# A macaron transformer block on one core: setup in pieces, loop in another order, z of the first groups made in the loop

## The reference

```python
def fp4_quant_dequant(x):
    xb = x.reshape(shape[:-1] + (shape[-1] // BLOCK, BLOCK))
    scale = jnp.max(jnp.abs(xb), axis=-1, keepdims=True) / 6.0
    scale = jnp.maximum(scale, jnp.float32(1e-12))
    idx = jnp.searchsorted(_MID, jnp.abs(xb / scale))
    q = _GRID[idx] * jnp.sign(xb / scale) * scale
...
h = silu(fp4_linear(x, w_gate)) * fp4_linear(x, w_up)   # 256 -> 704
ffn = fp4_linear(h, w_down)                             # 704 -> 256
...
x = x + 0.5 * ffn(layernorm(x))
x = x + attention(layernorm(x))     # causal softmax, one head, d = 256
x = x + 0.5 * ffn(layernorm(x))
```

## Time and profile before

| | |
|---|---|
| median of 3 runs | 1227.78 us (1227.09 to 1229.02) |
| the profiled execution | 1227.53 us, its span 1225.4 us |
| TensorE busy | 1160.7 us, 95% |
| VectorE busy | 1012.5 us, 83% |
| ScalarE busy | 789.4 us, 64% |
| GpSimd busy | 555.3 us, 45% |
| TensorE idle, 0 to 80 us | 36.8 us |
| TensorE idle, 360 to 440 us | 12.9 us |

### The profile page before, as it was taken

One profiled execution on the slowest core, in us unless ns is written; L12 is line 12 of the kernel. 1 busy time (PEld: TensorE's weight loads), 2 busy tenths in 40 slices (PEclk: granted clock), 3 DMA queues, 4 the chain that ended last, 5 costly groups with the idle time before them and its releaser, 6 DMA issues.

```text
span 1225.4 us, 24518 instructions
## 1 busy us (share of the span) xinstructions
PE 1160.7 (95%) x7765; PEld 758.2 (62%) x7765; DVE 1012.5 (83%) x2809; ACT 789.4 (64%) x1599; POOL 555.3 (45%) x531
## 2 busy tenths in 40 slices
PE   1799999999998889999999999999999999999997
PEld 1356666666665656676677667566666666666665
DVE  6899999999999676557556654764799999999996
ACT  4678888888864444435544453665678888888862
POOL 1445544545443344435443444445344544545532
PEclk9899999999999999999999999999999999999999
DMA  6955455444444456556573656547355555555565
GB/s 208 254 95 97 85 97 96 84 89 91 90 91 80 89 114 110 106 118 106 106 130 81 119 101 120 111 90 122 59 102 115 109 115 122 114 110 113 111 124 114
DMA packets 462740, 134.35 MB, mean 110 GB/s; under 512 B 441296, under 2 KB 461904, under 8 KB 462672
## 3 DMA queue, kind: packets, MB, share of 16 engines
q1 hardware_dynamic: 454928, 125.62, 52.9%
q10 hardware_dynamic: 7744, 7.86, 2.0%
HBM read 11.34 MB, written 8.39 MB: 16 GB/s over the span
## 4 chain that ended last, share of the span: by engine, by line
PE 75%; DVE 12%; issue 4%; ACT 3%; DMA 2%; SPq 2%; POOL 1%; DVEq 0%; ACTq 0%; POOLq 0%
PE ps L1512 32%; PE ps L1471 17%; PE ps L1559 12%; PE ps L1547 10%; PE ps L1532 2%; PE ps L1525 2%; DMA arena<-arena 2%; SPq L436 2%; DVE arena L1156 1%; DVE arena L1135 1%; DVE arena L991 1%; DVE arena L987 1%; ACT arena L815 1%; DVE arena L1048 1%; DVE arena L1143 1%
## 5 line engine op out<-in xcount | busy, mean ns | idle before, releaser
L1512 PE MATMUL ps<-wguT,arena 128*128 128x512 f16 (+1 forms) x2304 | 479.5, 363 | 4.4 <-DMA arena<-arena 3.2
L1512 PEld LDWEIGHTS ps<-wguT,arena 128*128 128x128 f16 x2304 | 226.0, 98 | 224.9 <-issue 7.2
L567 POOL TENSOR_TENSOR arena<-arena 128x704 f32<-128x704 f32 x128 | 193.6, 1512 | 248.1 <-DVE arena L1000 248.1
L1471 PE MATMUL ps<-wdT,arena 128*128 128x256 f16 x2176 | 261.3, 275 | 13.8 <-DMA arena<-arena 6.8
L1471 PEld LDWEIGHTS ps<-wdT,arena 128*128 128x128 f16 x2176 | 213.6, 98 | 55.1 <-DVE x_sb L1058 9.1
L594 POOL TENSOR_TENSOR arena<-arena 128x128 f16<-128x128 f32 (+7 forms) x64 | 144.0, 2250 | 213.8 <-ACT arena L815 138.7
L824 ACT ACTIVATE arena<-ps,arena,cst 128x128 f16<-128x128 f32 (+7 forms) x64 | 80.5, 1257 | 172.1 <-DVE arena L1161 149.3
L1559 PE MATMUL ps<-arena 128*128 128x256 f16 x1632 | 188.7, 273 | 1.6 <-DVE x_sb L1174 1.6
L1547 PE MATMUL ps<-arena 128*128 128x512 f16 (+3 forms) x960 | 187.2, 347 | 0.9 <-ACT arena L815 0.9
L1559 PEld LDWEIGHTS ps<-arena 128*128 128x128 f16 x1632 | 158.8, 98 | 26.8 <-DVE x_sb L1174 2.6
L745 ACT ACTIVATE arena<-arena 128x704 int16<-128x704 f32 x128 | 100.8, 787 | 114.2 <-POOL arena L567 114.2
(11 more groups left out here) (132 smaller groups left out, 1430.0 us busy)
## 6 DMA issues: line engine op xcount, KB each, us to landing
out_dram<-x_sb SPq DMA_DIRECT2D x32, 256.0 KB, 2.7
x_sb<-in_L_attn_x_dram ACTq DMA_DIRECT2D x3, 2048.0 KB, 9.1
arena<-arena SPq DMA_TRANSPOSE x384, 3.5
arena<-arena SPq DMA_DIRECT2D x8, 256.0 KB, 2.9
arena<-arena SPq DMA_DIRECT2D x4, 512.0 KB, 3.1
x_sb<-in_L_attn_x_dram ACTq DMA_DIRECT2D x1, 1536.0 KB, 7.3
arena<-in_L_ffn_w_down_dram SPq DMA_DIRECT2D x1, 704.0 KB, 8.5
arena<-in_L_ffn_w_gate_dram SPq DMA_DIRECT2D x1, 640.0 KB, 4.5
```

The lines of the kernel that those rows point to most:

```text
L567: g.tensor_tensor(hy[u].rearrange("p (j b) -> p b j", j=BL), h[u].rearrange("p (b j) -> p b j", j=BL), hri[u].unsqueeze(2).to_broadcast([P ...
L1471: i = nc.tensor.matmul(ps_dn[w % 2], hT[w][:, c * P:(c + 1) * P], wdT[:, k, :], start=(s == 0), stop=(s == len(DOWN_STEPS) - 1))
L1512: i = nc.tensor.matmul(psf[:, 1536 * u + lo:1536 * u + hi], xv[:, u, xl, kt, :], wguT[:, wl, lo // P:hi // P, kt, :], start=(s == 0), stop ...
```

## The change

It has these parts.

- **Setup in pieces.** Gate and up weights are loaded and quantized in three pieces (4, 4 and 3 tiles), VectorE starts when the first three gate tiles are there, and gate's maximum is found alone, ahead of up's, with one transpose for each column (four rounds in place of three) and without the scaled diagonal. ScalarE makes the codes of pieces 1 and 2 and of W_down, loads its silu table at the start, issues W_q, W_k and the first two pairs of x, and makes silu(0) within the setup. W_down's product and planes move from GpSimd to VectorE. TensorE's 40 and 24 idle products go.
- **x loads and transposes.** x is loaded pair by pair, from the SP queue, six pairs ahead; x's third transpose moves from before W_down's transposes to between their halves.
- **Query-key planes.** ScalarE copies m from PSUM to SBUF, so that its bank is free; `m_planes` and `wv_planes` move to after pairs 10 and 11.
- **Loop in another order.** `dve_pair`, `act_pair` and `pool_pair` get another order; the old one stays for the first two pairs of each FFN (`..._edge_pair`). The last 22 pairs of the first FFN are unrolled.
- **z made ahead.** Statistics, z and planes of groups 0, 1 and 2 are made in the loop, five pairs apart, from pairs 12, 17 and 22 on (`Z_PAIR`): z by ScalarE, the low plane by VectorE, the transposes one plane per pair.

The diff, cut to what matters:

```diff
-        W_PIECES = ((0, 6), (6, RT))
+        W_PIECES = ((0, 4), (4, 8), (8, RT))
...
+        Z_EARLY = 3
+        Z_PAIR = [NP - 20 + 5 * g for g in range(Z_EARLY)]
+
+        def tail_pairs(first, n):
+
+            return n if first else 22
...
             sp_w_T(0)
             sp_x_T(0, 0)
             sp_w_T(1)
+            sp_w_T(2)
             sp_x_T(1, 1)
-            sp_x_T(2, 0)
+            load_x(sp, 4)
+            load_x(sp, 5)
             sp.wait_ge(d_qhi, 2)
             sp.wait_ge(d_q, 2)
             for t in range(2):
                 for pl, c0, c1, w in ((0, 0, FW, WD_HI), (1, 0, FW, WD_LO), (0, FR, F, WD_HI_SHIFTED)):
                     sp.dma_start_transpose(wdT[:, w:w + (c1 - c0) // P, t * P:(t + 1) * P], dq16[:, pl, t, c0:c1]
                                            ).then_inc(d_T, 16)
+                if t == 0:
+                    sp_x_T(2, 0)
             for k in range(NP):
                 if k < NP - 2:
                     sp_pair(k, k % 2, first=(k == 0), x2=(k > 0))
+                    if k + 6 < NP:
+                        load_x(sp, k + 6)
                 else:
                     sp_h_T(2 * k - 1, (2 * k - 1) % 4)
-                    sp_z_T(k - (NP - 2))
                     sp_h_T(2 * k, 2 * k % 4)
+                for pl in range(2):
+                    if k - 9 - pl in Z_PAIR:
+                        sp_z_T(Z_PAIR.index(k - 9 - pl), (pl,))
             sp_h_T(NT - 1, 3)
+            sp_z_T(Z_EARLY - 1, (1,))
...
+        def pool_pair(gp, odd, x3=True, x4=True, z1=False):
+            static = isinstance(gp, int)
+            if x4 and not static:
+                pool_x_var(gp + 4, odd)
+            pool_h_y(2 * gp, 0)
+            if x4:
+                if static:
+                    pool_x_var(gp + 4, odd)
+                pool_x_root(gp + 4)
+            if z1:
+                pool_z_lo(1)
+            pool_h_y(2 * gp + 1, 1)
+            if x3:
+                pool_x_y(gp + 3)
+            if x4:
+                pool_x_shift(gp + 4, odd)
...
+        def act_pair(gp, p, odd, start=None, x2=True, x3=True, x4=True, z1=False, loaded=None):
+            a = 2 * gp
+            if loaded is not None:
+                nc.scalar.wait_ge(ld_x[2 + odd], loaded)
+            if not (isinstance(gp, int) and gp == 0):
+                act_silu(a, 0)
+            if start != 0:
+                act_h_n(a - 1, 1)
+            if x4:
+                act_x_mean(gp + 4, p + 4, odd)
+            if start != 0:
+                act_h_c(a - 1, 1)
+            act_silu(a + 1, 1)
+            if start != 0:
+                act_h_fc(gp - 1, 1 - odd)
+            if z1:
+                act_load_table(ACT.Exp)
+            if x4:
+                act_x_squares(gp + 4, p + 4, odd)
+            if x3:
+                act_x_z(gp + 3, p + 3)
+            if x2:
+                act_x_n(gp + 2)
+                act_x_c(gp + 2)
+            act_h_n(a, 0)
+            act_h_c(a, 0)
+
+        def act_z(g, half):
+
+            nc.scalar.wait_ge(z_nm, g + 1)
+            if g >= 1 and not half:
+                nc.scalar.wait_ge(z_lo, g)
+            for t in range(2 * half, 2 * half + 2):
+                i = nc.scalar.activation(zf.rearrange("p (k t c) -> p t k c", k=KT, t=GT)[:, t],
+                                         x_sb[:, (g * GT + t) * D:(g * GT + t + 1) * D].rearrange("p (k c) -> p k c", k=KT),
+                                         ACT.Identity, bias=znm[:, t:t + 1], scale=zru[:, t:t + 1])
+            if half:
+                i.then_inc(z_z, 1)
...
+            load_x(act, 0)
+            act.wait_ge(consts_made, 1)
+            act_load_table(ACT.Silu)
             act.wait_ge(ld_x[0], 16)
             act_x_mean(0, 0, 0)
             act_x_squares(0, 0, 0)
...
+            for dst, src, ld in ((wq_raw, wq_in, ld_q), (wk_raw, wk_in, ld_k)):
+                act.dma_start(dst.rearrange("p (t k) -> p t k", t=KT),
+                              src.rearrange("(t p) k -> p t k", p=P)).then_inc(ld, 16)
+            load_x(act, 1)
             act_x_z(0, 0)
             w_n_part(0)
...
+            act.wait_ge(ld_x[1], 16)
+            act_x_mean(1, 1, 1)
+            act_x_squares(1, 1, 1)
             act_x_n(0)
+            act_x_c(0)
             for e, dst in enumerate((wqT, wkT)):
                 act.wait_ge(qk_tr, e + 1)
                 nc.scalar.activation(dst, ps[:, 5 + e, :], ACT.Copy).then_inc(qk_ev, 1)
...
             act_x_z(1, 1)
+            w_n_part(1)
+            act.wait_ge(w_c, 1)
+            w_c_part(1)
+            w_n_part(2)
+            w_c_part(2)
+            act_x_n(1)
+            act.wait_ge(m_done, 1)
+            nc.scalar.activation(wqT, ps_m, ACT.Copy).then_inc(m_raw, 1)
+            act.wait_ge(ld_x[2], 16)
+            act_x_mean(2, 2, 0)
+            act_x_c(1)
+            act_x_squares(2, 2, 0)
+            act_x_z(2, 2)
+            act_silu(0, 0)
             act.wait_ge(d_y, 1)
             nc.scalar.activation(dn.rearrange("p (t j b) -> p t j b", t=2, j=BL),
                                  dy.rearrange("p (t b j) -> p t j b", t=2, j=BL), ACT.Copy, scale=CELLS, bias=-0.5
                                  ).then_inc(d_n, 1)
...
+            act.wait_ge(d_n, 1)
+            nc.scalar.activation(dn.bitcast(f16), dn, ACT.Copy, scale=0.25 * CODE, bias=0.125 * CODE).then_inc(d_c, 1)
+            act.wait_ge(ld_x[3], 16)
             act_x_mean(3, 3, 1)
             act_x_squares(3, 3, 1)
...
+        def dve_pair(gp, qd, p, odd, start=None, x2=True, x3=True, end=False, adds=False):
+
+            a = 2 * gp
+            if start != 0 or gp != 0:
+                dve_h_rin(a, 0)
+            if x2:
+                dve_x_sh(gp + 2)
+            dve_h(a + 1, 1)
+            if start is None:
+                dve_res(gp - 2, odd, 0, p * 2 - 4)
+            if adds:
+                dve_last_add(TB - 2)
+            dve_h_amax(a + 1, 1)
+            if x2:
+                dve_x_sl(gp + 2)
+            dve_h_s(a + 1, 1)
+            if start != 0:
+                dve_h_q(gp - 1, 1, quad(qd, 2 * odd - 3))
+            dve_h_rin(a + 1, 1)
+            if x2:
+                dve_x_g(gp + 2)
+            if x3:
+                dve_x_amax(gp + 3)
+            dve_h_max(gp)
+            if not end:
+                dve_h(a + 2, 0)
+            if x3:
+                dve_x_s(gp + 3)
+            dve_h_pow(gp)
+            dve_h_g(a, 0)
+            dve_h_inv(gp)
+            if x2:
+                dve_x_q(gp + 2, 0, (qd + odd, 1 - odd))
+                dve_x_q(gp + 2, 1)
+            dve_h_sp(gp)
+            if x3:
+                dve_x_rin(gp + 3)
+            dve_h_sd(gp)
+            if not end:
+                dve_h_amax(a + 2, 0)
+            if start is None:
+                dve_res(gp - 2, odd, 1, p * 2 - 3)
+            if adds:
+                dve_last_add(TB - 1)
+            dve_h_sh(gp)
+            if x3:
+                dve_x_sd(gp + 3)
+            if not end:
+                dve_h_g(a + 1, 1)
+            dve_h_sl(gp)
+            if not end:
+                dve_h_s(a + 2, 0)
+            dve_h_q(gp, 0, quad(qd, 2 * odd - 2))
...
+            dve.wait_ge(ld_gate, 16)
+            w_amax_part(0, 3)
+            dve.wait_ge(ld_gate_b, 16)
+            dve.wait_ge(ld_mid, 32)
+            w_amax_part(3, FT + 1)
             dve.wait_ge(w_amax, 2)
...
+            w_scale(0)
+            column_peak(0, wam[:, 0:gt])
+            column_peak(1, wam[:, gt:gt + XB])
+            w_rinv(0)
             w_y_part(0)
...
+            dve_x_amax(0)
+            find_peaks(0)
+            dve_x_s(0)
+            dve_x_rin(0)
+            dve.wait_ge(ld_up, 16)
+            w_amax_part(FT + 1, RT)
+            norm_floor(0)
+            dve.wait_ge(w_amax, 3)
+            column_peak(2, wam[:, gt + XB:NB1])
+            norm_pow(0)
+            w_scale(1)
+            norm_inv(0)
+            w_code(0)
+            norm_factors(0)
+            normed(0)
+            V.tensor_scalar(wsp[:, 0:a_end], wsc[:, 0:a_end], gup[:, 0:1], None, ALU.mult).then_inc(w_sp, 1)
+            dve_x_sd(0)
+            w_diff(0)
+            w_grid(0)
+            w_hi(0)
+            dve_x_sh(0)
+            w_lo(0)
+            dve_x_sl(0)
+            w_q_part(0)
+            dve_x_g(0)
+            w_rinv(1)
+            dve_x_q(0, 0)
+            dve_x_q(0, 1)
+            find_peaks(1)
             w_y_part(1)
...
+            norm_floor(1)
+            w_y_part(2)
+            norm_pow(1)
+            dve_x_amax(1)
+            norm_inv(1)
+            dve_x_s(1)
+            norm_factors(1)
+            normed(1)
+            for r, c, k in ((slice(0, P), slice(a_end, gt), 0), (slice(0, FR), slice(gt, gt + XB), 0),
+                            (slice(FR, P), slice(gt, gt + XB), 1), (slice(0, P), slice(gt + XB, NB1), 1)):
                 V.tensor_scalar(wsp[r, c], wsc[r, c], gup[r, k:k + 1], None, ALU.mult).then_inc(w_sp, 1)
...
```

(81 more changed lines are left out.)

411 lines of the change are left out of this document (197 added, 214 removed).

## The result

The changed kernel takes 1220.95 us (median of 5 runs, 1217.85 to 1222.89), the kernel before 1227.78 beside it; the ratio is 0.9939, with an interval of 0.9922 to 0.9957. It is faster, as forecast, but 6.8 us are gained where 22.8 were expected, and the time lies outside the range of 1197 to 1215. The profiled execution of the changed kernel is its fastest, 1217.85, 3.1 us under the median; its span is 1215.8 us (1225.4 before). One execution of a later run, `b2_new_order`, took 2062.39 us at a granted clock of 0.56 and stands in none of the ratios.

A forecast was written before the change was run, and what follows sets the result against it. TensorE was taken to bound the loop, with VectorE also full, so gains come from setup and the passage into attention: 9.0 + 13.8 = 22.8, and 1227.5 - 22.8 = 1204.7 us, range 1197 to 1215.

The forecast's parts named there:

- setup, to two down tiles done: Setup until six gate/up and two down tiles are done: 10.9 us earlier, less 1.9 charged, net 9.0 gained.
- loop, 320.6 before: First FFN's loop: 5.3 us gained from three waits and slow clock at its end, 1.0 lost to plane work.
- edits at nothing: Small edits and new waits across the kernel put at 0, among them ScalarE's waits for x loads.
- sign of being wrong: In the loop: the forecast would be wrong if VectorE's pair took over 10.84 us.
- The room in the loop: First FFN's loop: the new order frees 0.8 us of VectorE a pair, 17.4 of room against 12.4 added work.
- A (it only moves): Rival, loop: the 0.8 us stall only moves, a pair stays at 10.84; +9.5, or 1214; chance 0.16.
- C (VectorE becomes the bound): Rival, loop: x's grid waits behind GpSimd's product, a pair takes 11.3 us; 1242 in all; chance 0.06.
- charge of 1.9 for the clock: Setup: 1.9 us (0 to 6) charged for TensorE products at the low clock after gaps.
- Rival B: Setup gives only 4 us because TensorE's clock is low behind every gap; 1210; chance 0.18.
- The passage: From the first FFN loop's end into attention: shorter tail and fewer waits for z and statistics, 9.5 us gained.
- The term for the first FFN's tail: Last gate/up product to the end of the idle products: 12.5 us instead of 15.1, 2.6 gained.
- The charge of 1.3: Start of attention: 1.3 us (0 to 3) lost to late softmax steps of slots 3 to 5.

The follow-up runs named there:

- b2_new_order: The kernel before with only the new order of the rolled loops on VectorE, ScalarE and GpSimd; 1228.54 us without the slow execution, ratio 1.0004.
- e3_z_early: The changed kernel with ScalarE's x-load wait moved behind the silu and the early groups' z transposes one pair earlier; 1206.48 us, ratio 0.9832.
- e9_factor_behind_squares: e3_z_early with ScalarE's residual factor put back behind the squares of x in the new order; 1207.91 us, ratio 0.9841.

## Why the prediction was wrong, by its own steps

The profiled executions, 1225.4 us of span before, 1215.8 with the change and 1207.1 with both causes removed (`e3_z_early`), split like this (us gained):

| step | forecast | measured | with both causes removed |
|---|---|---|---|
| setup, to two down tiles done | 9.0 | 9.2 | 7.5 |
| loop, 320.6 before | 4.3 (5.3 - 1.0) | -7.7 | 3.5 |
| from there to the end, 828.7 before | 9.5 | 8.3 | 7.6 |

(The loop is measured from the second down product's start, the first row to its end; from its start it is 9.0 and 7.3, and the columns then add up to 9.6 and 18.4, where the spans differ by 9.6 and 18.3. The 7.5 belongs to an execution with a slow first down product; in `e9_factor_behind_squares` the same stretch gained 10.0.)

- **The step that failed** is one clause among the edits at nothing: "ScalarE waits for x loads, issued six pairs ahead: 0." Six is a difference of indices. The load of pair k+6 goes out when VectorE ends pair k, and there ScalarE is about to begin pair k+2, which reads x pair k+6 and whose first silu was made to wait for it. In time the load is ahead by half a pair: 5.65 us from the quantization's end to h, and that is filled by 1.4 of transpose issue, 3.2 from the start of the load's issue to its landing, 0.85 of silu and 0.2 between them. The prediction put the wait at nothing without working out this time. The runs showed a closed loop of 11.1 us a pair against TensorE's 10.84, for 7.1 us in all (6.5 in the loop, 5.0 by the ratios). The prediction's own sign of being wrong, a VectorE pair of over 10.84, did appear (11.11), but with 0.96 us of idling in front of h in it, so not by VectorE's work.
- **The second one** was not seen at all: the parts named the wait for the high z plane by the low one, but not the high plane of group g waiting for the transposes of group g-1, the last of which SyncE issues in the pair five after the one in which group g's statistics begin, while ScalarE writes at the end of the pair six after it; it runs ahead of SyncE by more than a pair, so that is the same moment (306.05 and 309.85 in the rows above). Cost 5.2 alone, 7.4 behind the first (3.9 and 4.7 in the loop).
- In the loop the forecast missed by 12.0 us (+4.3 against -7.7), and with both removed 11.2 of them are back. By the medians it is 14.5 of 16.3 (13.1 by the ratios); the time is then 1206.48, 1.8 from the forecast of 1204.7.
- **The room in the loop** was right in kind and nearly in size: 0.69 us a pair (forecast 0.8). Rivals A (it only moves) and C (VectorE becomes the bound) are out: VectorE's busy time itself fell, with both causes removed TensorE waits 1.5 us in all from 80 to 396, and L1132, the former L1022, takes 243 ns in the changed kernel. The Trainium skill (SBUF — State Buffer, section SBUF: two separate sides) says that the port pair shared by VectorE and GpSimd is held for a whole instruction by whoever starts first; the product that took 1050 ns before and 243 once its place in the order had changed agrees with that. What the room is worth is 6.5 us, where rival A had put the lack of it at 9.5.

```profile
L1132 DVE TENSOR_TENSOR arena<-arena 128x88 f32<-128x88 f32 x18 | 4.4, 243 | 0.0
```

- **The setup** came out nearly as worked out: the first down product at 61.69 for 60, so 9.2 us earlier where the working gave 10.9 before its charge of 1.9 for the clock. That the total is met is in part luck: the charge was for slow products, and those of tile 1 were hardly on the path, while the chain of VectorE came about a microsecond later than worked out, as in these starts of h(1) to h(3) for 47.1, 52.2 and 56.8:

```profile
48.22 0.94 DVE L1097 SCALAR_TENSOR_TENSOR arena<-ps,cst,arena 128x704 f32<-128x704 f32 x1
53.23 0.94 DVE L1097 SCALAR_TENSOR_TENSOR arena<-ps,cst,arena 128x704 f32<-128x704 f32 x1
57.84 0.93 DVE L1097 SCALAR_TENSOR_TENSOR arena<-ps,cst,arena 128x704 f32<-128x704 f32 x1
```

- **Rival B** (the clock low behind every gap) is out, both that the clock is low behind every gap and that it costs as much. Tile 1 did run at 1.2 GHz for most of its 6.23 us, but curing it gave nothing. Only a slow first down product costs something, and only in some executions: from its start to the next one it is 6.89 us with both causes removed (61.94 to 68.83) and 5.43 with idle products ahead of it. The Trainium skill (TensorE: Matmul & The Clock Gate, section HAM oscillation) has TensorE fall back to half rate in a wait, if the wait is long enough. The prediction left that condition out when it said "each gap" and when it saw a disagreement at 38.56. The runs agree in that both levels appear behind gaps. They do not sort by the length of the gap just ahead: 2.52 us gave the low level at 61.94 (3.50 us for 17 products), 2.87 the full rate at 55.83, and 3.15 the full rate too, in the run with the load issued earlier:

```profile
61.95 2.02 PE L1751 MATMUL ps<-wdT,arena 128*128 128x256 f16 x17 [3.15 <-DMA arena<-arena]
```

- **The passage** was forecast at 9.5 and gave 8.3. The term for the first FFN's tail is exact: from the last gate/up product to the end of the idle products 12.5 us for 15.1, 2.6 gained. Short by 1.1 is what comes behind. The charge of 1.3 for what would be late next named the softmax steps; what came were the waits of 0.25, 0.48 and 1.34 shown above, the last for group 3's transposes, which the prediction does not name. The second FFN's tail was put within 0.3; these are its three waits, longer by 0.44, shorter by 0.63 and longer by 0.32 than the 0.72, 2.53 and 2.22 of before, and from the end of its last gate/up product to its last down products it is 0.1 longer:

```profile
1198.69 2.02 PE L1751 MATMUL ps<-wdT,arena 128*128 128x256 f16 x17 [1.16 <-DMA arena<-arena]
...
1202.60 2.02 PE L1751 MATMUL ps<-wdT,arena 128*128 128x256 f16 x17 [1.90 <-DMA arena<-arena]
...
1207.16 5.54 PE L1751 MATMUL ps<-wdT,arena 128*128 128x256 f16 x34 [2.54 <-DMA arena<-arena]
```

What stays open: 1.8 us between the best run and the forecast, and whether the executions of the changed kernel scatter more than those of the kernel before: five of each spread over 5.0 and 1.9 us, but 17 of the kernel before on another chip over 4.2. A wait for a transfer within the closed loop would make each late landing count, but with the wait moved the spread was no smaller, so no run shows this.

## What to carry to other kernels

Measure the lead of a prefetch in time and not in iterations: from the event that lets it be issued to the instruction that waits for it, counting the issues queued ahead of it and its landing, and then see whether that wait and that event lie on one closed loop; if they do, the loop's sum against the bound engine's period decides, and not the wait's length. Put a wait directly ahead of the instruction that needs it, since whatever stands between becomes part of that loop. And a new order that frees an engine can tighten such a loop at the same time: the same wait cost nothing in one order and 5 to 7 us in the other.

## What the runs showed of the hardware

- ScalarE's queue can wait 15.3 us in 16 places (paced loads in the kernel before) and the kernel's loop stays at 320.6 us; a list of waits shows where an engine stood, not what it cost.
- TensorE's clock is not told by the gap alone: after 2.13 us of idling the first down product ran at full rate in the changed kernel (2.02 us for 17), after 2.52 with both causes removed at the low one for most of it (3.50), after 2.87, ahead of 55.83, at full rate again (3.74 for 18), and after 3.15 at full rate (2.02 for 17, the load issued earlier). In the two runs with idle products of 2.35 us in the two late gaps, all four stretches behind them ran at full rate.
- A load of 256 KB took 3.2 us (median) from the start of its issue to its landing, 0.77 of it issue on SyncE's queue, in a kernel that uses 57% of the DMA engines' time over its span.
